# A vision-transformer block on one core: the order of the work in its first 45 microseconds is rearranged

## The chip, the cores and the metric

The kernel runs on one core of a Trainium2 chip. The core has a matrix engine (PE in the profile, with its weight loads as PEld), a vector engine (DVE, VectorE), a scalar engine (ACT, ScalarE), GpSimd (POOL) and a queue that only starts transfers (SP). The metric is the device time of one execution in microseconds; lower is better.

## The reference

The input is 16 images of 3 x 96 x 96. Each gives 36 patches of 768 values; with a class token an image has 37 rows of 256 values. Three steps follow. Only the first bears on this change.

```python
def tok(x, weight, class_token, pos_embedding):
    xn = patches * rsqrt(mean(patches * patches) + 1e-6)          # rms norm, per row
    scale = 127 / clip(max(abs(xn)), 1e-5)                        # per row
    xq = clip(round(xn * scale), -128, 127) / scale
    wscale = 1 / clip(mean(abs(weight)), 1e-5)                    # one number for all 256 x 768 weights
    wq = clip(round(weight * wscale), -1, 1) / wscale             # ternary weights
    return concat([class_token, xq @ wq.T]) + pos_embedding
h = tok(x)
h = h + attention(layernorm(h))        # 16 heads, rotary numerator, plain denominator, causal, + bout
h = h + mixture(layernorm(h))          # 8 heads of attention; one of 8 experts per row for values and outputs
```

## The kernel before

Every engine has its own program, written out by hand in order, and the engines meet in semaphores. The 592 rows (16 x 37) are worked in six groups of three images (111 rows; the last has one image). A group is one tile of `xp`, and group g is "g" everywhere below.

**The front (0 to 37 us).** SP starts all loads at once, in a fixed order: group 0, the identity (`ident`), group 1, the token weights `tw` (128 x 1536), groups 2 and 3, the other constants, the small vectors, groups 4 and 5, then the later weights. Per group:
- ScalarE squares and sums (`square`, L552), GpSimd makes the reciprocal root (`rrms`, a power, L451), VectorE takes the absolute maximum (`absmax`, L788), and from both VectorE makes the scales in three tiny steps (`quant_scales`, L801 to L805).
- ScalarE multiplies and rounds by adding a large number (`round_up`, L558). VectorE takes that number off again and clips into bf16 (`quantised`, L813). TensorE transposes the result (`turn_q`, L1153), ScalarE copies it out of PSUM (`quantised_T`, L567), TensorE multiplies with the ternary weights (`embed` on TensorE, L1164), and VectorE scales, adds the position row and takes the statistics of the layer norm (`embed` on VectorE, L836 to L819).
- GpSimd makes the reciprocal deviation (L471), VectorE normalises (`ln_apply`, L828), TensorE transposes (`turn_x`, L1173), ScalarE keeps a rounded copy (`x1_hi`, L572) and VectorE the remainder (`x1_lo`, L845).

The ternary weights need the sum of all absolute weights first: VectorE sums along each partition (L857), TensorE adds the 128 partitions (`total_job`, L1140), VectorE scales and clips `tw` in two passes (L862, L863), and ScalarE takes the rounding number off (L624, tile `tern`). No product of `embed` on TensorE starts before `tern`.

**After the front.** The first projection jobs (`proj_job`, L267 to L269) start between the last groups' `turn_x`, in the order of the list `START`. ScalarE copies their results out of PSUM (L597, L606), VectorE applies the rotary tables in four rounds (`rope`, L913 to L920), and from the second round on TensorE makes scores and the attention (L1249 to L1289). The mask of the numerator is added by a product: `keys_bf` (an identity placed twice, in bf16) times `ahead_bf` (L1249); VectorE makes both in `ahead`, ahead of the first `rope`. GpSimd adds the attention's output bias `bout` to `h` (L485), then makes the lower halves of the second stage's weights (`w2_lo`, L466), one after each round of `rope`; VectorE's `residual` (L966) waits for the bias to be in.

Of the kernel before, what the change touches and what calls it, by code (L numbers as in the profile page):

```python
# [9 lines left out]
ACT = mybir.ActivationFunctionType  # L10
AX = mybir.AxisListType.X
F32 = mybir.dt.float32
F32R = mybir.dt.float32r
BF16 = mybir.dt.bfloat16
# [99 lines left out]
def vit_block(nc, x, tokw, vecs, consts, wqkv, wout, w2, ve, oe, mask_rows, out):  # L114
    with ExitStack() as ctx:
# [9 lines left out]
        gate_sel = sbuf(ctx, "gate_sel", [NH2 * NE, NH2, DH2], F32R)  # L125
        ones = sbuf(ctx, "ones", [P, P])
        half_neg = sbuf(ctx, "half_neg", [P, GI])
        h = sbuf(ctx, "h", [R, G, D])
# [49 lines left out]
        ropex = sbuf(first, "ropex", [P, 2, QH])  # L178
        keys_bf = sbuf(first, "keys_bf", [P, 2, DH2], BF16)
        ahead_bf = sbuf(first, "ahead_bf", [P, 2 * KC * JS, S], BF16)  # L180
# [167 lines left out]
        def groups_of(t):  # L348

            return -(-min((t + 1) * P, T) // R)  # L350

        START = [("turn", 0), ("turn", 1), ("total", 0), ("bias", 0), ("turn", 2), ("embed", 0), ("turn", 3), ("embed", 1),
                 ("turn", 4), ("embed", 2), ("turn", 5), ("x", 0), ("embed", 3), ("x", 1), ("embed", 4), ("x", 2),
# [80 lines left out]
        def _(pool):  # L434
# [47 lines left out]

            pool.wait_ge(sm["x1lo_ready"], G)
            for g in range(G):
                pool.tensor_tensor(h[:, g], h[:, g], biasb[:, 1], ALU.add).then_inc(sm["h0b_ready"], 1)  # L485
            for n in range(4):
                pool.wait_ge(sm["rope_t"], RSTEPS * (n + 1))
                w2_lo(n)

            def ve_lo(e):  # L490
# [55 lines left out]
        def _(act):  # L546
# [70 lines left out]
            quantised_T(0)  # L617
            round_up(1)
            square(2)
            square(3)  # L620
# [3 lines left out]
            act.activation(tern[:], tw[:], ACT.Copy, bias=-ROUND).then_inc(sm["tern_ready"], 1)  # L624
            round_up(2)
            square(5)
            bias_rows()
            quantised_T(2)
            round_up(3)
            round_up(4)  # L630
            quantised_T(3)
            round_up(5)
# [144 lines left out]
        def _(dve):  # L777
# [53 lines left out]
            def embed(g):  # L831
                dve.wait_ge(sm["proj_ps"], g + 1)
                if g == 0:
                    dve.wait_ge(sm["bias_sb"], 1)
                    dve.wait_ge(sm["dqs_ready"], 1)
                step("h0_ready", dve.scalar_tensor_tensor(  # L836
                    out=h[:, g], in0=ps[0:R, 2 + g % 2, 0:D], scalar=dqs[:, g:g + 1], in1=biasb[:, 0],
                    op0=ALU.mult, op1=ALU.add))
                ln_stats(0, g)
# [7 lines left out]


            absmax(0)
            dve.wait_ge(ident_in, 16)  # L850
            dve.tensor_copy(ident_bf[:], cols("ident")).then_inc(sm["ident_ready"], 1)
            quant_scales([0])
            absmax(1)
            quantised(0)
            quant_scales([1])
            dve.wait_ge(tokw_in, 16)
            dve.tensor_reduce(small[:, 0:1], tw[:], AX, ALU.add, apply_absolute_value=True).then_inc(sm["wabs"], 1)  # L857
            quantised(1)
            dve.wait_ge(sm["tot_ps"], 1)
            step("wscale", dve.tensor_scalar(small[:, 1:2], ps[:, 6, 0:1], 1.0 / (D * DIN), Q_EPS, ALU.mult, ALU.max))  # L860
            step("wscale", dve.reciprocal(small[:, 2:3], small[:, 1:2]))
            step("clip_t", dve.tensor_scalar(tw[:], tw[:], small[:, 2:3], 1.0, ALU.mult, ALU.min))  # L862
            dve.tensor_scalar(tw[:], tw[:], -1.0, ROUND, ALU.max, ALU.add).then_inc(sm["tern_pre"], 1)  # L863
            absmax(2)
            quant_scales([2])
            absmax(3)
            quant_scales([3])
            quantised(2)
            step("wscale", dve.tensor_scalar(small[:, 3:4], small[:, 1:2], 1.0 / 127.0, None, ALU.mult))
            absmax(4)  # L870
            absmax(5)
            quant_scales([4, 5])
            dve.tensor_scalar(dqs[:], amc[:], small[0:R, 3:4], None, ALU.mult).then_inc(sm["dqs_ready"], 1)
            quantised(3)
            embed(0)
            quantised(4)
# [19 lines left out]
            def rope(r):  # L896
# [22 lines left out]
                for j in range(2):  # L919
                    many(dve.tensor_scalar(krot[:, c, im, DH2 * j:DH2 * j + S], tmp[:, 1], cols("par")[:, j:j + 1],  # L920
                                           None, ALU.mult))

            def ahead():

                dve.memset(keys_bf[:], 0.0).then_inc(sm["ahead_ready"], 1)
                dve.tensor_copy(ahead_bf[:], bcast(cols("ahead"), 1, 2 * KC * JS)).then_inc(sm["ahead_ready"], 1)
                dve.wait_ge(sm["ahead_ready"], 1)
                for r in range(RT):
                    rows = slice(r * P // RT, r * P // RT + S)
                    dve.tensor_copy(keys_bf[rows, :, 0:S],  # L930
                                    bcast(cols("ident")[rows, rows], 1, 2)).then_inc(sm["ahead_ready"], 1)

# [195 lines left out]
        def _(pe):  # L1128
# [55 lines left out]
            def proj_job(n):  # L1184
# [27 lines left out]
                ins.then_inc(sm["proj1_ps"], 1)  # L1212

            for what, n in START:
                if what == "turn":
                    turn_q(n)
                elif what == "total":
                    total_job()
                elif what == "bias":
                    bias_job()  # L1220
                elif what == "embed":
                    embed(n)
                elif what == "x":
                    turn_x(n)
                else:
                    proj_job(n)
# [371 lines left out]
```

## Time and profile before

| | us |
|---|---|
| median of three runs | 235.15 |
| the three runs | 233.58, 235.15, 235.27 |
| the profiled execution, its own time | 234.06 |
| its span, first to last instruction | 232.3 |
| PE busy in the span | 204.3 (88%) |
| DVE busy in the span | 175.1 (75%) |
| ACT busy, POOL busy | 93.4 (40%), 78.7 (34%) |

The profile is of one execution; the 1.76 us between its span and its own time lie around the instructions. Engine time counts as busy from an instruction's start to its end, so an engine that is busy 88% of the span is not at its peak. A row of the timeline gives start, duration, engine, line, operation and, in brackets, the idle time ahead of it and what ended that.

### The profile page before, as it was taken

The page shows a single profiled execution, that of the slowest core. Times are in us where ns is not written, and L with a number is a line of the kernel's source. Part 1 is how long each engine was busy: PE and PEld are TensorE (multiplying, and loading weights), DVE is VectorE, ACT ScalarE, POOL GpSimd, SP SyncE. Part 2 cuts the span into 40 slices and gives each one's busy share as a digit, 9 for nine tenths or more (in the row PEclk, how much of TensorE's full clock was granted, in tenths as well). Part 3 has the DMA queues.
Part 4 walks back from the last instruction along what each step waited for, and adds up shares of the span by engine and source line. Part 5 has one row for each costly group of instructions (what it writes and reads, how often), then busy time and mean ns, then how long its engine had stood idle before and what let it go on. Part 6 is the DMA issues. An engine that isn't in the chain of part 4 may idle for free.

```text
span 232.3 us, 5174 instructions
## 1 busy us (share of the span) xinstructions
PE 204.3 (88%) x2095; PEld 178.0 (77%) x2095; DVE 175.1 (75%) x320; ACT 93.4 (40%) x184; POOL 78.7 (34%) x82
## 2 busy tenths in 40 slices
PE   0153879979998999999999999999999999999994
PEld 0032759978785989977687787679989999899993
DVE  1679896998868669825466766676799979979972
ACT  3578837986643463453412606247003021110000
POOL 8552575422206124005065294767460000000000
PEclk9999988999999999999999999999999999999998
DMA  6999000000000200005320043094024425522003
GB/s 188 248 271 378 11 0 4 0 3 3 3 3 3 90 4 0 0 3 157 128 92 4 0 171 102 1 259 134 0 62 164 151 71 195 177 75 77 28 3 106
DMA packets 7183, 19.57 MB, mean 84 GB/s; under 512 B 1044, under 2 KB 1879, under 8 KB 7031
## 3 DMA queue, kind: packets, MB, share of 16 engines
q1 hardware_dynamic: 7158, 19.24, 26.3%
q8 instruction: 17, 0.28, 0.5%
q14 instruction: 8, 0.06, 0.1%
HBM read 18.55 MB, written 0.68 MB: 83 GB/s over the span
## 4 chain that ended last, share of the span: by engine, by line
PE 50%; DVE 29%; issue 8%; POOL 4%; ACT 4%; DMA 4%; SPq 1%; DVEq 0%; ACTq 0%; POOLq 0%
PE ps L267 12%; PE ps L268 11%; PE ps L269 11%; DVE gx L1117 8%; PE ps L1260 4%; DMA tw<-tok_weight 4%; PE ps L1473 2%; DVE oelo L1091 2%; DVE rden L947 2%; DVE amax L788 2%; PE ps L1443 1%; ACT ptb L734 1%; POOL velo L495 1%; PE ps L1276 1%; DVE stat L817 1%
## 5 line engine op out<-in xcount | busy, mean ns | idle before, releaser
L1117 DVE TENSOR_TENSOR gx<-maskb,oT 128x1184 fp32r<-128x1184 bf16 x31 | 42.3, 1410 | 0.6 <-PE ps L269 0.5
L1054 DVE COPY_PREDICATED v<-onehot,ps 128x512 f32<-128x512 uint8 (+3 forms) x40 | 25.7, 660 | 17.6 <-PE ps L269 17.3
L267 PE MATMUL ps<-gx,oelo 128*128 128x296 f32 x124 | 37.8, 305 | 0.6 <-DVE gx L1117 0.6
L269 PE MATMUL ps<-gx,oehi 128*128 128x296 f32 x124 | 37.2, 300 | 0.0
L268 PE MATMUL ps<-gx,oehi 128*128 128x296 f32 x124 | 36.9, 298 | 0.0
L267 PE MATMUL ps<-vehi,x2lo 128*128 128x512 f32 (+3 forms) x90 | 35.3, 392 | 0.0
L268 PE MATMUL ps<-velo,x2hi 128*128 128x512 f32 (+3 forms) x90 | 33.4, 371 | 0.0
L269 PE MATMUL ps<-vehi,x2hi 128*128 128x512 f32 (+3 forms) x90 | 33.2, 369 | 0.0
L495 POOL TENSOR_TENSOR velo<-veraw,vehi 128x1024 fp32r<-128x1024 f32 x8 | 19.1, 2390 | 20.4 <-ACT vehi L672 16.1
L267 PEld LDWEIGHTS ps<-gx,oelo 128*128 128x128 f32 x124 | 23.3, 188 | 1.8 <-issue 1.2
L268 PEld LDWEIGHTS ps<-gx,oehi 128*128 128x128 f32 x124 | 23.4, 189 | 0.0
L269 PEld LDWEIGHTS ps<-gx,oehi 128*128 128x128 f32 x124 | 23.3, 188 | 0.0
L267 PEld LDWEIGHTS ps<-vehi,x2lo 128*128 128x128 f32 (+1 forms) x90 | 16.2, 180 | 4.3 <-issue 0.7
L1153 PE MATMUL ps<-ident_bf,qb 111*128 111x111 bf16 x36 | 4.2, 282 | 17.2 <-DVE qb L813 17.2
L269 PEld LDWEIGHTS ps<-vehi,x2hi 128*128 128x128 f32 (+1 forms) x90 | 16.2, 180 | 3.7
L268 PEld LDWEIGHTS ps<-velo,x2hi 128*128 128x128 f32 (+1 forms) x90 | 16.2, 180 | 2.8
L1153 PEld LDWEIGHTS ps<-ident_bf,qb 111*128 111x128 bf16 x36 | 2.9, 131 | 18.9 <-DVE qb L813 18.8
L471 POOL TENSOR_TENSOR rstd<-lnv,half_neg 111x1 f32<-111x1 f32 x12 | 7.8, 649 | 24.7 <-DVE lnv L819 24.7
L742 ACT ACTIVATE oehi<-oeraw 128x1024 fp32r<-128x1024 f32 x8 | 8.5, 1064 | 18.9 <-DMA oeraw<-output_w 17.8
L721 ACT ACTIVATE pe<-sc 101x444 f32<-101x444 f32 (+1 forms) x6 | 3.2, 534 | 24.5 <-POOL sc L510 24.5
L267 PE MATMUL ps<-x2hi,w2lo 128*128 128x222 f32 (+1 forms) x32 | 10.4, 324 | 0.0
L947 DVE RECIPROCAL rden<-ps 128x296 f32<-128x296 f32 x4 | 8.0, 1991 | 3.1 <-PE ps L1289 3.1
(169 smaller groups left out, 471.5 us busy)
## 6 DMA issues: line engine op xcount, KB each, us to landing
maskb<-mask_rows SPq DMA_DIRECT2D x32, 148.0 KB, 3.5
veraw<-value_w SPq DMA_DIRECT2D x8, 512.0 KB, 3.6
oeraw<-output_w SPq DMA_DIRECT2D x8, 512.0 KB, 3.9
xp<-x_rows SPq DMA_DIRECT2D x6, 336.0 KB, 9.5
w2raw<-w_qkgate SPq DMA_DIRECT2D x1, 1088.0 KB, 14.8
tw<-tok_weight SPq DMA_DIRECT2D x1, 768.0 KB, 8.1
wqraw<-w_qkv SPq DMA_DIRECT2D x1, 768.0 KB, 12.7
out<-yo SPq DMA_DIRECT2D x4, 148.0 KB, 1.9
```

The lines of the kernel that those rows point to most:

```text
L267: pe.matmul(o, llo, rhi, start=start, stop=False)
L268: pe.matmul(o, lhi, rlo, start=False, stop=False)
L269: return pe.matmul(o, lhi, rhi, start=False, stop=stop)
L471: pool.tensor_tensor(rstd[:, which, g:g + 1], lnv[:, which, g:g + 1], half_neg[0:R, 0:1], ALU.pow).then_inc(sm["rstd_ready"], 1)
L495: pool.tensor_tensor(velo[:, e % NVR], veraw[:, e % NVR], vehi[:, e % NVR].bitcast(F32), ALU.subtract).then_inc(sm["velo_ready"], 1)
L742: act.activation(oehi[u % NOR][:], oeraw[RAW[u]][:], ACT.Copy).then_inc(sm["oehi_ready"], 1)
L788: dve.tensor_reduce(amax[:, g:g + 1], xp[0:R, g], AX, ALU.max, apply_absolute_value=True).then_inc(sm["amaxed"], 1)
L947: dve.reciprocal(rden[:], ps[:, DENB[b], 0:UN * S]).then_inc(sm["rden_ready"], 1)
L1054: dve.copy_predicated(v2[0:m, t, h0:h1], bcast(onehot[0:m, t, h0:h1, e], 2, DH2), ps[0:m, JBANK[n], 0:(h1 - h0) * DH2].rearrange("p (a b) ...
L1117: dve.tensor_tensor(gx[:, k % NGR].rearrange("p a b t -> p a (b t)"), bcast(maskb[:, w % NMR, k % MEU], 1, 2), oT[:, c % 2].bitcast(F32), ...
L1153: ins = pe.transpose(dst[:, c * (R + 1):c * (R + 1) + R], qb[:, g % NQB, c * P:(c + 1) * P], ident_bf[0:R, 0:R])
L1260: ins = pe.matmul(ps[0:QR, 2 * t + r, o:o + JS * S], key, qry, start=kind == 1, stop=kind == 1 or (ii, c) == (1, KC - 1))
```

## The change

- VectorE's sum of the absolute weights becomes a ScalarE pass (`Abs` with an accumulator) between `round_up(1)` and `square(2)`; its elementwise result goes into `tern`, which a later step overwrites.
- `absmax(2)` and `absmax(3)` move ahead of VectorE's wait for the total; the scales of groups 2 and 3 are made together; `quantised(3)` moves ahead of `embed(0)`, and `embed(0)` ahead of the scales of groups 4 and 5. `dqs` is made in two parts.
- On ScalarE `round_up(3)` moves to just behind `round_up(2)`, and `quantised_T(3)` to behind `quantised_T(2)`.
- `keys_bf` is made early, in a function of its own, `ahead_keys`, ahead of the scales of group 1.
- TensorE multiplies the identity by itself eight times behind the bias products, into a PSUM bank that nobody reads before it is written again; `embed(0)` comes ahead of `turn_q(2)`.
- GpSimd's six additions of `bout` move behind the four `w2_lo`, and no longer wait for `x1lo_ready`.

```diff
-        START = [("turn", 0), ("turn", 1), ("total", 0), ("bias", 0), ("turn", 2), ("embed", 0), ("turn", 3), ("embed", 1),
+        START = [("turn", 0), ("turn", 1), ("total", 0), ("bias", 0), ("warm", 8), ("embed", 0), ("turn", 2), ("turn", 3), ("embed", 1),
...
-            pool.wait_ge(sm["x1lo_ready"], G)
-            for g in range(G):
-                pool.tensor_tensor(h[:, g], h[:, g], biasb[:, 1], ALU.add).then_inc(sm["h0b_ready"], 1)
             for n in range(4):
                 pool.wait_ge(sm["rope_t"], RSTEPS * (n + 1))
                 w2_lo(n)
+            for g in range(G):
+                pool.tensor_tensor(h[:, g], h[:, g], biasb[:, 1], ALU.add).then_inc(sm["h0b_ready"], 1)
...
             round_up(1)
+            act.wait_ge(tokw_in, 16)
+            act.activation(tern[:], tw[:], ACT.Abs, accum_out=small[:, 0:1]).then_inc(sm["wabs"], 1)
             square(2)
...
             round_up(2)
+            round_up(3)
             square(5)
             bias_rows()
             quantised_T(2)
-            round_up(3)
+            quantised_T(3)
             round_up(4)
-            quantised_T(3)
             round_up(5)
...
+            def ahead_keys():
+                dve.memset(keys_bf[:], 0.0).then_inc(sm["ahead_ready"], 1)
+                dve.wait_ge(sm["ahead_ready"], 1)
+                for r in range(RT):
+                    rows = slice(r * P // RT, r * P // RT + S)
+                    dve.tensor_copy(keys_bf[rows, :, 0:S],
+                                    bcast(cols("ident")[rows, rows], 1, 2)).then_inc(sm["ahead_ready"], 1)
...
             quantised(0)
+            ahead_keys()
             quant_scales([1])
-            dve.wait_ge(tokw_in, 16)
-            dve.tensor_reduce(small[:, 0:1], tw[:], AX, ALU.add, apply_absolute_value=True).then_inc(sm["wabs"], 1)
             quantised(1)
+            absmax(2)
+            absmax(3)
             dve.wait_ge(sm["tot_ps"], 1)
...
             dve.tensor_scalar(tw[:], tw[:], -1.0, ROUND, ALU.max, ALU.add).then_inc(sm["tern_pre"], 1)
-            absmax(2)
-            quant_scales([2])
-            absmax(3)
-            quant_scales([3])
-            quantised(2)
+            quant_scales([2, 3])
             step("wscale", dve.tensor_scalar(small[:, 3:4], small[:, 1:2], 1.0 / 127.0, None, ALU.mult))
             absmax(4)
+            quantised(2)
+            dve.tensor_scalar(dqs[:, 0:4], amc[:, 0:4], small[0:R, 3:4], None, ALU.mult).then_inc(sm["dqs_ready"], 1)
+            quantised(3)
             absmax(5)
+            embed(0)
             quant_scales([4, 5])
-            dve.tensor_scalar(dqs[:], amc[:], small[0:R, 3:4], None, ALU.mult).then_inc(sm["dqs_ready"], 1)
-            quantised(3)
-            embed(0)
+            dve.tensor_scalar(dqs[:, 4:G], amc[:, 4:G], small[0:R, 3:4], None, ALU.mult).then_inc(sm["dqs_ready"], 1)
             quantised(4)
...
+            def keep_clock(n, bank):
+
+                for _ in range(n):
+                    pe.matmul(ps[:, bank, 0:P], cols("ident"), cols("ident"), start=True, stop=True)
```

`ahead()` keeps its place but makes only `ahead_bf`.

## Rows read from the trace of the kernel before

**Rows 1.** The chain of waits: start us, us, what
```profile
10.27 1.75 DVE small L857
...
19.79 1.82 DVE amax L788 x2
...
25.28 0.50 DVE h L836
...
41.22 1.31 DVE ropex L915
```

**Rows 2.** Timeline of ScalarE, front
```profile
10.01 0.94 ACT L558 ACTIVATE xp<-xp,qsc 111x768 f32<-111x768 f32 x1 [0.27 <-DVE qsc L805]
...
12.94 0.84 ACT L552 ACTIVATE sqjunk<-xp 111x768 f32<-111x768 f32 x1 [0.36 <-DMA xp<-x_rows]
...
15.68 0.84 ACT L552 ACTIVATE sqjunk<-xp 111x768 f32<-111x768 f32 x1 [1.19 <-DMA xp<-x_rows]
...
16.52 1.47 ACT L624 ACTIVATE tern<-tw 128x1536 bf16<-128x1536 f32 x1
17.90 0.92 ACT L558 ACTIVATE xp<-xp,qsc 111x768 f32<-111x768 f32 x1
```

**Rows 3.** Timeline of VectorE, front
```profile
9.37 0.21 DVE L801 TENSOR_SCALAR amc<-amax,rrms 111x1 f32<-111x1 f32 x1 [1.19 <-POOL rrms L451]
...
13.66 0.16 DVE L860 TENSOR_SCALAR small<-ps 128x1 f32<-128x1 f32 x1 [1.17 <-PE ps L1140]
...
15.11 0.96 DVE L863 TENSOR_SCALAR tw<-tw 128x1536 f32<-128x1536 f32 x1
...
21.71 0.34 DVE L801 TENSOR_SCALAR amc<-amax,rrms 111x1 f32<-111x1 f32 x2
...
22.61 0.55 DVE L813 TENSOR_SCALAR qb<-xp 111x768 bf16<-111x768 f32 x1
23.08 0.48 DVE L836 SCALAR_TENSOR_TENSOR h<-ps,dqs,biasb 111x256 f32<-111x256 f32 x1
...
24.35 0.56 DVE L813 TENSOR_SCALAR qb<-xp 111x768 bf16<-111x768 f32 x1
```

**Rows 4.** Timeline of GpSimd
```profile
14.24 1.86 POOL L451 TENSOR_TENSOR rrms<-msq,half_neg 111x1 f32<-111x1 f32 x1
...
37.66 4.22 POOL L485 TENSOR_TENSOR h<-h,biasb 111x256 f32<-111x256 f32 x6 [2.53 <-DVE x1lo L845]
...
58.40 1.34 POOL L466 TENSOR_TENSOR w2lo<-w2raw,w2hi 128x544 fp32r<-128x544 f32 x1 [3.78 <-DVE krot L920]
```

**Rows 5.** Timeline of TensorE
```profile
14.22 2.04 PE L1133 MATMUL ps<-vrow,cst 3*111 3x256 f32 x4 [0.60 <-DMA cst<-constants]
...
20.28 1.49 PE L1164 MATMUL ps<-tern,qT 128*111 128x256 bf16 x6
...
27.75 0.82 PE L1164 MATMUL ps<-tern,qT 128*111 128x256 bf16 x6
...
49.15 0.33 PE L1249 MATMUL ps<-ahead_bf,keys_bf 37*101 37x296 bf16 x2 [1.33 <-DVE krot L920]
```

**Rows 6.** Window: length; busy PE, PEld, DVE, ACT, POOL; granted clock; DMA share; GB/s
```profile
34.00:35.00 1.00, 1.00 (x6) 0.91 (x5) 0.95 (x4) 0.28 (x1) 0.54 (x1) 0.50 0.00 0
```

**Rows 7.** Timeline of VectorE from 35 us
```profile
35.17 0.41 DVE L828 TENSOR_SCALAR xhat<-h,mv,rstd 111x256 f32<-111x256 f32 x1
...
37.73 1.43 DVE L930 CAST keys_bf<-cst 37x74 bf16<-37x74 f32 x2
39.49 0.01 DVE L913 LOAD_MASK_SELECT partner<-ps  x1 [0.33 <-ACT kun L597]
```

**Rows 8.** Line L1173 of TensorE, timeline
```profile
36.68 0.36 PE L1173 MATMUL ps<-cst,xhat 111*128 111x111 f32 x2
```

**Rows 9.** VectorE's second rotary round and first residual, timeline
```profile
46.05 0.77 DVE L915 TENSOR_TENSOR ropex<-partner,cst 128x592 f32<-128x592 f32 x1
...
68.92 0.41 DVE L966 TENSOR_TENSOR h<-h,ps 111x256 f32<-111x256 f32 x1
```

More of the change, by code:

```diff
@@ L126, in vit_block @@
         ones = sbuf(ctx, "ones", [P, P])
+        keys_bf = sbuf(ctx, "keys_bf", [P, 2, DH2], BF16)
         half_neg = sbuf(ctx, "half_neg", [P, GI])
@@ L178, in vit_block @@
         ropex = sbuf(first, "ropex", [P, 2, QH])
-        keys_bf = sbuf(first, "keys_bf", [P, 2, DH2], BF16)
         ahead_bf = sbuf(first, "ahead_bf", [P, 2 * KC * JS, S], BF16)
@@ L835, in embed @@
                     dve.wait_ge(sm["dqs_ready"], 1)
+                elif g == 4:
+                    dve.wait_ge(sm["dqs_ready"], 2)
                 step("h0_ready", dve.scalar_tensor_tensor(
@@ L846, in x1_lo, with ahead @@
                                   hi.bitcast(F32), ALU.subtract).then_inc(sm["x1lo_ready"], 1)
+            def ahead():
+                dve.tensor_copy(ahead_bf[:], bcast(cols("ahead"), 1, 2 * KC * JS)).then_inc(sm["ahead_ready"], 1)
+            def ahead_keys():
[5 more added lines that the diff above has]
+                                    bcast(cols("ident")[rows, rows], 1, 2)).then_inc(sm["ahead_ready"], 1)
             absmax(0)
@@ L921, in rope @@
                                            None, ALU.mult))
[L923 to L931, printed above, removed]
             ahead()
@@ L1220, in _ @@
                     bias_job()
+                elif what == "warm":
+                    keep_clock(n, 4)
                 elif what == "embed":
```

## The prediction

> **What bounds the kernel now.** I read the chain of waits first, because this change shortens no large group of work: it reorders the front. The chain enters the front through VectorE's sum of the absolute weights at 10.27 us, stays on VectorE through the maxima of the groups and the additions of the embedding, and leaves through ScalarE's copies into VectorE's rotary rounds [rows 1]. Then I read the timelines of the engines next to each other, for what ends each pause. Two things decide the rest. ScalarE starts `tern` at 16.52, the moment its squares of group 4 are through, and those waited for group 4's transfer until 15.68 [rows 2]; VectorE had the clipped weights ready at 15.11 + 0.96 = 16.07 [rows 3]. So the weight path has 0.45 us of slack ahead of a transfer. And from 18 to 25 us ScalarE's rounding and VectorE's order hold each other up: the bf16 groups 3 and 4 come out at 22.61 and 24.35 only [rows 3], though ScalarE could round group 2 at 17.90 [rows 2].
>
> **The sum of the weights.** It leaves VectorE (1.75 us) [rows 1] for ScalarE. I price the pass by `tern`, which reads the same 128 x 1536 in 1.47 us [rows 2]. ScalarE is through with `round_up(1)` at 10.01 + 0.94 = 10.95, so the sum is there at about 12.45 (a little more for reading the accumulator), against 10.27 + 1.75 = 12.02 before. The total reached VectorE 1.64 us after the sum (13.66) [rows 3], with TensorE's transposes of group 1 in between; by that the new total arrives at the latest at 14.1. Now the two maxima ahead of that wait: group 3 landed at 12.94 [rows 2] and a maximum takes 1.82 / 2 = 0.91 [rows 1], so VectorE reaches the wait at 13.9. The clipping starts at 13.9 to 14.1 instead of 13.66 and ends 2.41 later, at 16.3 to 16.5. `tern` still starts at 16.52. Queued behind the pass on ScalarE are the squares of groups 2 and 3; they come 0.8 and 0.4 us later, and nothing needs them before 16.3. Gain of this part to here: nothing; group 4's transfer ends the wait in both orders.
>
> [...]
>
> **What follows from 16.5 us.** This is where the gain is. The joint scales of groups 2 and 3 take what those of 4 and 5 took together, 22.61 - 21.71 = 0.9 [rows 3], and need GpSimd's power for group 3. GpSimd's power beside the clipping took 1.86 us and ended with it at 16.10 [rows 4]; if it is held so again, until 16.5, the scales are there at 17.4, ahead of the end of `tern` (16.52 + 1.47 = 17.99). So ScalarE can run `round_up(2)` and `round_up(3)` back to back from 17.9, done at 18.8 and 19.75 at 0.92 each [rows 2]. VectorE: `quantised(2)`, then `quantised(3)` at 19.8 (before: 22.61), 0.55 to 20.35, `absmax(5)` to 21.25, `embed(0)` at 21.25 (before: 23.08) for 24.35 - 23.08 = 1.27, to 22.5 [rows 3]. But now the scales of groups 4 and 5 stand behind `embed(0)`: 22.5 + 0.9 = 23.4 at most, the part that ScalarE needs 0.1 earlier, so `round_up(4)` runs 23.3 to 24.2 and `quantised(4)` 24.2 to 24.75 (before: 24.35). `embed(1)` follows at 24.7; before it waited for TensorE until 25.28 [rows 1]. Of the 1.8 us at `embed(0)` 0.6 are left there; from there VectorE's loop of normalise, embed, statistics is the same as before. **Gain 0.6.**
>
> **The eight products.** They fill TensorE between the bias products' end, 14.22 + 2.04 = 16.26, and `embed(0)` [rows 5]. They are not in the trace. The nearest row is the bias, float32 as well: 512 columns in four records for 2.04. By columns the eight (1,024 columns) take 4.1 us, by records (16) 8.2, and at the doubled clock half of either: 2.0 to 8.2. I take 3 to 4, by columns with the clock risen on the way, for the rows are alike in that a column count sets them. They end at 19.3 to 20.3, `embed(0)` takes 0.82 at the high and 1.49 at the low clock [rows 5], and is done at 20.1 to 21.8; VectorE wants it at 21.25. Cost: nothing to 0.5; I take nothing, because `absmax(5)` covers it, and price the rest as a rival. `turn_q(2)` and `turn_q(3)`, now behind `embed(0)`, are needed by `embed(2)` after 25 us only.
>
> **The clock.** At 27.75 `embed` takes 0.82 and at 20.28 1.49, the ratio of 2.4 to 1.2 GHz [rows 5], though the clock column says full speed in both places; I go by the durations. In the window from 34 to 35 us the granted clock is 0.50, TensorE at 1.2 GHz under the first projection jobs [rows 6], after a stretch in which it only served `embed` group by group. Group 5 was normalised at 35.17 + 0.41 = 35.58 [rows 7], its transposes started at 36.68, behind those slow jobs [rows 8]: 1.1 us of the path. Forecast: the clock falls again, as TensorE's work from 25 to 32 us is unchanged, and this neither gains nor loses.
>
> **The mask's identity.** `keys_bf` (a memset and two casts, 1.43 together) leaves its place ahead of the rotary rounds. There it earns nothing by itself: VectorE waited another 0.33 for ScalarE's copy of the keys [rows 7]. In the new place it fills a pause of 1.19 [rows 3]; at 1.6 in all it would run 0.4 over, and the 0.4 goes into the weights' slack. The rotary rounds therefore follow ScalarE, which is 0.6 earlier.
>
> **The additions of `bout`.** Their six 0.7 us steps run from 37.66 to 41.88 [rows 4]. VectorE's L915, two operands from SBUF, starts at 41.22 and takes 1.31 on the chain [rows 1]; the same step of the next round, with GpSimd idle, takes 0.77 [rows 9]. The difference goes: **gain 0.5**, and TensorE, which paused 1.33 for VectorE at 49.15 [rows 5], can follow. In the new place the additions run behind the last `w2_lo` (58.40 + 1.34), to 64.0; `residual(0)` needs them at 68.92 [rows 4, 9], so 4.9 us of cover. VectorE reads PSUM beside them there. A second collision as large would cost 0.5; I take nought. `dqs` in two parts adds an instruction of some 0.2 in a pause: nought.
>
> **Sum.** 0.6 + 0.5 = 1.1 off the span: 232.3 to 231.2, and with the 1.76 around it 234.06 becomes 232.96. The median of the runs is 235.15, 1.1 above that execution, which would give 234.05. The two ends of the shown runs are as far apart as the gain, so I take the middle, 233.5.
>
> **Rivals**, each from the same middle of 234.6.
> - *The clock stays high into the projection jobs.* For it: eight products at the start of TensorE's work give it a rise earlier than 26 us; against it: the pauses from 25 to 32 remain. Up to 1.1 more, of which six products stand between the transposes anyway: 0.8. 232.7. The Trainium skill (TensorE: Matmul & The Clock Gate, "What's actually happening") says that the low clock is the default and activity releases it, which speaks for a rise at the eight products but not for its lasting.
> - *The eight products hold `embed(0)` up*, and the kernel is slower. Place: TensorE between 16.26 and `embed(0)`. At the middle of the two prices, 6.1 us, they end at 22.4, `embed(0)` near 23.5, and all that hangs on it is 2.2 later than in the forecast: 1.1 slower than before, 235.7. It decides from 21 us on: a later end than that takes the whole 1.1. Against it: TensorE is then busy from 14.2 without a pause, and under the projection jobs, just as dense, the clock rose again.
> - *Half of it does not arrive.* ScalarE's copies are only 0.6 earlier; if they and not VectorE set the first masked scores, the 0.5 is lost: 234.0. Against it: TensorE's 1.33 of waiting for VectorE.
>
> **How the numbers follow.** Forecast 0.56 (232.9 to 234.1), clock 0.18, half 0.16, slower 0.10. The range leaves out a tenth at each end: from 231.5, a little under the clock case counted from the profiled execution (234.06 - 1.1 - 1.1 = 231.9), to 235.8, which takes in the slow case's middle. A measurement here tells about 1% from no change; 1% below 235.15 is 232.8. Below it lies more than half of the clock case and a quarter of the forecast: 0.25. Above 237.5 lies only the end of the slow case: 0.06. Within: 0.69.
>
> **What would show it.** `tern` still at about 16.5; `quantised(3)` near 19.8; VectorE's first `embed` near 21.3 and the second near 24.7; L915 at 0.8 in both first rounds; `rope` starting 0.6 earlier, the first masked scores 1.1 earlier, and that distance kept to the end. I would be wrong if group 3 landed later than 13.2, for then the clipping waits for its maximum and `tern` moves one for one; if `Abs` brought a table load to ScalarE; or if the clock's rise and fall moved by more than the 1.1.

## The result, and the profile after

| us | before | changed |
|---|---|---|
| median (11 runs each) | 234.54 | 231.56 |
| lowest to highest | 232.92 to 237.74 | 230.99 to 234.74 |
| ratio of the two, 95% interval | | 0.9877 [0.9846, 0.9907] |

The kernel became 1.2% faster: 2.9 us, by the interval 2.2 to 3.6. The forecast was 1.1. Its direction was right and the time lies in its range, but the gain is more than twice the sum, and "faster by over 1%" had been given 0.25. Ratios, here and below, leave out executions that are more than 1.5% above the fastest of their kernel; medians and ranges take in all.

The profiled execution of the changed kernel is one of its longer ones (234.74 us, span 232.9), because TensorE ran at the low clock from 84 to 91 us, as shown below; up to 84 us its rows are held against those of before step by step.

The front first. ScalarE's timeline in the changed kernel answers to [rows 2]:

```profile
11.04 1.47 ACT L619 ACTIVATE tern<-tw 128x1536 bf16<-128x1536 f32 x1
12.41 0.19 ACT L619 ACTIVATION_READ_ACCUMULATOR tern<-tw 128x1 f32 x1
...
15.54 0.85 ACT L551 ACTIVATE sqjunk<-xp 111x768 f32<-111x768 f32 x1 [0.68 <-DMA xp<-x_rows]
16.41 1.48 ACT L625 ACTIVATE tern<-tw 128x1536 bf16<-128x1536 f32 x1
17.80 1.75 ACT L557 ACTIVATE xp<-xp,qsc 111x768 f32<-111x768 f32 x2
```

The new pass takes what `tern` takes. `tern` still starts when the squares of group 4 are through, and those still wait for a transfer: 16.41 against 16.52. Behind it the two roundings now stand together. VectorE's timeline, answering to [rows 3, 7] and to L915 on the chain of [rows 1]:

```profile
8.48 0.46 DVE L861 CAST keys_bf<-cst 37x74 bf16<-37x74 f32 x2
...
13.98 0.15 DVE L876 TENSOR_SCALAR small<-ps 128x1 f32<-128x1 f32 x1
15.42 0.96 DVE L879 TENSOR_SCALAR tw<-tw 128x1536 f32<-128x1536 f32 x1
19.58 0.56 DVE L814 TENSOR_SCALAR qb<-xp 111x768 bf16<-111x768 f32 x1
20.95 0.48 DVE L839 SCALAR_TENSOR_TENSOR h<-ps,dqs,biasb 111x256 f32<-111x256 f32 x1
24.50 0.48 DVE L839 SCALAR_TENSOR_TENSOR h<-ps,dqs,biasb 111x256 f32<-111x256 f32 x1
38.32 0.01 DVE L927 LOAD_MASK_SELECT partner<-ps  x1 [1.69 <-ACT kun L596]
39.85 0.78 DVE L929 TENSOR_TENSOR ropex<-partner,cst 128x592 f32<-128x592 f32 x1
```

`quantised(3)` comes at 19.58 (before 22.61), `embed(0)` at 20.95 (23.08), `embed(1)` at 24.50 (25.28): of 2.13 us, 0.78 are left at the second. The first rotary round, with GpSimd now idle beside it, takes 0.78 in the step that took 1.31 on the chain. TensorE's timeline:

```profile
16.02 3.51 PE L1221 MATMUL ps<-cst 128*128 128x128 f32 x16
19.37 0.82 PE L1168 MATMUL ps<-tern,qT 128*111 128x256 bf16 x6
35.51 0.35 PE L1177 MATMUL ps<-cst,xhat 111*128 111x111 f32 x2
55.73 1.04 PE L1287 MATMUL ps<-en,vblk 101*32 101x37 f32 x64
```

The eight products end at 19.53, and the first `embed` is over before VectorE wants it. The transposes of group 5 start at 35.51, not at 36.68 [rows 8], and the 64 attention products run in one piece. That last row has to be held against two of the kernel before, which the prediction had not read:

```profile
57.60 0.76 PE L1276 MATMUL ps<-en,vblk 101*32 101x37 f32 x63
58.87 0.19 PE L1276 MATMUL ps<-en,vblk 101*32 101x37 f32 x1 [0.50 <-issue]
```

There TensorE stood still for 0.50 us ahead of the last of the 64, and waited for nothing that the profile shows ("issue"). After it comes the second attention's denominator. VectorE's timeline, the first two denominators of the kernel before, then of the changed one:

```profile
58.40 1.95 DVE L947 RECIPROCAL rden<-ps 128x296 f32<-128x296 f32 x1
...
61.73 2.01 DVE L947 RECIPROCAL rden<-ps 128x296 f32<-128x296 f32 x1 [0.88 <-PE ps L1289]
```

```profile
56.53 1.95 DVE L951 RECIPROCAL rden<-ps 128x296 f32<-128x296 f32 x1
...
59.35 2.01 DVE L951 RECIPROCAL rden<-ps 128x296 f32<-128x296 f32 x1 [0.37 <-PE ps L1300]
```

They are 3.33 us apart before and 2.82 after.

Three windows of the changed kernel, answering to [rows 6]:

```profile
26.00:27.00 1.00, 0.61 (x7) 0.62 (x8) 1.00 (x3) 0.46 (x1) 1.00 (x2) 0.50 0.02 8
34.00:35.00 1.00, 0.63 (x5) 0.63 (x6) 0.86 (x3) 0.18 (x1) 0.67 (x1) 1.00 0.00 0
...
87.00:88.00 1.00, 1.00 (x5) 1.00 (x4) 0.97 (x2) 0.18 (x1) 0.20 (x1) 0.50 0.00 0
```

Full speed (2.4 GHz) is now granted under the first projection jobs, where it was 0.50 (1.2 GHz) before; but 0.50 came at 26 us, where TensorE serves `embed` group by group, and again at 84 to 91 us, under dense products that follow some pauses. Where the time went in this pair of profiles:

| step, start us | before | after | sum of gain |
|---|---|---|---|
| VectorE `embed(1)` | 25.28 | 24.50 | 0.78 |
| VectorE `embed(3)` | 29.24 | 28.83 | 0.41 |
| `x1_hi(5)` | 37.08 | 35.90 | 1.18 |
| `ropex` of the second round | 46.05 | 44.16 | 1.89 |
| first denominators | 58.40 | 56.53 | 1.87 |
| second denominators | 61.73 | 59.35 | 2.38 |
| first memset of `sc` | 87.30 | 84.89 | 2.41 |
| `gmT` of the first expert | 98.42 | 98.96 | -0.54 |

The order brings 0.78; the low clock under TensorE's `embed(3)` goes with a loss of 0.37; full clock under the projection jobs brings 0.77; the rotary round 0.5, and 0.2 more in the steps just ahead of it; the missing pause 0.5. Then the low clock at 84 us takes 2.95. Without that stretch this execution would have had some 234.06 - 2.41 = 231.65, close to the median of 231.56. So two things are to be settled: what the eight products do, and whether the clock is part of the change.

### The profile page after: what moved, and what is told of

It is laid out like the page before. It is cut to its first block, busy times and chain, and to the rows that moved or that the text cites. A ratio compares the mean times of both kernels' runs of the same rounds, so it can differ in the third digit from the quotient of the medians.

```text
span 232.9 us, 5208 instructions
## 1 busy us (share of the span) xinstructions
PE 208.2 (89%) x2111; PEld 182.3 (78%) x2111; DVE 171.9 (74%) x320; ACT 94.5 (41%) x186; POOL 78.5 (34%) x82
## 4 chain that ended last, share of the span: by engine, by line
PE 49%; DVE 25%; issue 8%; ACT 6%; DMA 4%; POOL 4%; SPq 2%; DVEq 0%; ACTq 0%; POOLq 0%
PE ps L267 12%; PE ps L268 11%; PE ps L269 11%; DVE gx L1121 8%; DMA xp<-x_rows 4%; PE ps L1271 4%; PE ps L1484 2%; DVE oelo L1095 2%; DVE rden L951 2%; PE ps L1454 1%; ACT ptb L735 1%; ACT xp L557 1%; DVE stat L818 1%; POOL velo L494 1%; PE ps L1287 1%
## 5 line engine op out<-in xcount | busy, mean ns | idle before, releaser
L1058 DVE COPY_PREDICATED v<-onehot,ps 128x512 f32<-128x512 uint8 (+3 forms) x40 | 25.7, 659 | 17.7 <-PE ps L269 17.4
L267 PEld LDWEIGHTS ps<-gx,oelo 128*128 128x128 f32 x124 | 23.3, 188 | 1.8 <-issue 1.3
L269 PEld LDWEIGHTS ps<-gx,oehi 128*128 128x128 f32 x124 | 23.3, 188 | 0.0
L1157 PE MATMUL ps<-ident_bf,qb 111*128 111x111 bf16 x36 | 3.4, 255 | 14.9 <-DVE qb L814 14.9
L466 POOL TENSOR_TENSOR w2lo<-w2raw,w2hi 128x544 fp32r<-128x544 f32 x4 | 5.4, 1352 | 17.7 <-DVE krot L934 17.7
L267 PE MATMUL ps<-x2hi,w2lo 128*128 128x222 f32 (+1 forms) x32 | 11.4, 355 | 0.0
```

What stands on the lines that cost most here:

```text
L267: pe.matmul(o, llo, rhi, start=start, stop=False)
L269: return pe.matmul(o, lhi, rhi, start=False, stop=stop)
L466: pool.tensor_tensor(w2lo[:, n // 2, part], w2raw[:, n // 2, part], w2hi[:, n // 2, part].bitcast(F32), ALU.subtract).then_inc(sm["w2lo_re ...
L1058: dve.copy_predicated(v2[0:m, t, h0:h1], bcast(onehot[0:m, t, h0:h1, e], 2, DH2), ps[0:m, JBANK[n], 0:(h1 - h0) * DH2].rearrange("p (a b) ...
L1157: ins = pe.transpose(dst[:, c * (R + 1):c * (R + 1) + R], qb[:, g % NQB, c * P:(c + 1) * P], ident_bf[0:R, 0:R])
```

## The experiments

Letters in the expectations: **theory A** says that the eight products earn by the clock under the projection jobs; **theory C** that they earn only because 32 more TensorE instructions (16 matmul records and their weight loads) move the pause. The rival to both is the prediction's sum, in which the products earn nothing. Each ratio is against the kernel before on the same chip. Since the low clock falls in different places from execution to execution, the place of each low stretch is told, and in places the lowest spans stand beside the medians. Diffs are against the changed kernel unless another is named; of a long list they show the part that changes, and `...` stands for lines left out.

**1. Without the eight products.**

```diff
-  ("total", 0), ("bias", 0), ("warm", 8), ("embed", 0), ("turn", 2),
+  ("total", 0), ("bias", 0), ("embed", 0), ("turn", 2),
```

> The changed kernel without the eight products. Theory A (the eight products decide where TensorE's clock is low later, and kept it high under the first projection jobs): the low stretch of some 3.4 us returns under the first two projection jobs, group 5's transposes come about 1 us later behind their normalised rows, and the time is 0.6 to 1.1 us above the changed kernel's, a ratio to the kernel before of 0.990 to 0.992. Theory B (the products only raise the clock for the first two embeddings, for which nothing waits; where the clock falls later is drawn anew in each execution): the time is within 0.3 us of the changed kernel's, a ratio of 0.987 to 0.989, and the low stretch is anywhere between 25 and 40 us.

Measured: 233.08 us, ratio 0.9888 [0.9856, 0.992], not told apart from the 0.9877 of the changed kernel. The clock was low at 25.1 to 28.5 us and full under the projection jobs, without the products. For the new order theory A falls by that. The pause in the attention products is back, and larger. TensorE's timeline of this kernel:

```profile
55.49 0.76 PE L1287 MATMUL ps<-en,vblk 101*32 101x37 f32 x63
57.05 0.19 PE L1287 MATMUL ps<-en,vblk 101*32 101x37 f32 x1 [0.80 <-issue]
```

From the first to the second denominators it takes 3.62 us; the changed kernel, 2.82. So the trace gives the products 0.80 here. Its shortest span is 229.6 and that of the changed kernel, on two chips, 229.1.

**2. The kernel before with the eight products alone** (diff against before):

```diff
-  ("bias", 0), ("turn", 2), ("embed", 0),
+  ("bias", 0), ("warm", 8), ("turn", 2), ("embed", 0),
...
```

> The kernel before, with nothing but the eight products added between the bias products and the transposes of group 2. Theory A: the clock is high under the first projection jobs, and the time falls by 0.6 to 1.1 us (ratio 0.995 to 0.997). Theory B: ratio 0.999 to 1.001, as the first embedding was not what VectorE waited for. In both, the products take about 3.5 us from 16.2 on and the first embedding then takes 0.82 instead of 1.49.

Measured: 234.14, ratio 0.9918 [0.9876, 0.9959], a larger gain than either theory had said, though the interval reaches theory A's. No pause; 2.80 us between the denominators, where the kernel before takes 3.33. The rotary step L915 still takes 1.27. The clock was low at 23.3 to 26.7 and 84.8 to 88.2, and full under the projection jobs. And VectorE's `embed(1)` comes at 24.52, which is not the pause's doing. Run 10 below is this kernel with products that do next to nothing, and its `tern` starts at the same time (15.77, here 15.74). TensorE's timeline here, then TensorE's and VectorE's of run 10:

```profile
22.86 0.47 PE L1153 MATMUL ps<-ident_bf,qb 111*128 111x111 bf16 x6 [2.11 <-DVE qb L813]
23.16 1.32 PE L1164 MATMUL ps<-tern,qT 128*111 128x256 bf16 x6
```

```profile
22.89 0.74 PE L1153 MATMUL ps<-ident_bf,qb 111*128 111x111 bf16 x6 [1.45 <-DVE qb L813]
23.42 1.49 PE L1164 MATMUL ps<-tern,qT 128*111 128x256 bf16 x6
...
24.95 0.48 DVE L836 SCALAR_TENSOR_TENSOR h<-ps,dqs,biasb 111x256 f32<-111x256 f32 x1 [0.37 <-PE ps L1164]
```

In the old order VectorE waits there for TensorE. The faster transposes and products save 0.43, the full clock under the projection jobs makes it 1.12 at `x1_hi(5)` (35.65 against 36.77), and 1.25 are left at the second denominators. In this pair, then, the products earn by the clock as well, as theory A says. In the new order TensorE is through with `embed(1)` at 21.43 in the changed kernel, three microseconds ahead of VectorE, and that wait is gone.

**3. The order alone**: no products, the additions of `bout` and `ahead_keys` in their old places.

```diff
-  ("bias", 0), ("warm", 8), ("embed", 0),
+  ("bias", 0), ("embed", 0),
...
+            pool.wait_ge(sm["x1lo_ready"], G)
+            for g in range(G):
+                pool.tensor_tensor(h[:, g], h[:, g], biasb[:, 1], ALU.add).then_inc(sm["h0b_ready"], 1)
             for n in range(4):
...
-            for g in range(G):
-                pool.tensor_tensor(h[:, g], h[:, g], biasb[:, 1], ALU.add).then_inc(sm["h0b_ready"], 1)
...
             quantised(0)
-            ahead_keys()
             quant_scales([1])
...
+            ahead_keys()
             ahead()
```

> The kernel before with only the order of the front changed: the sum of the weights on ScalarE, the maxima of groups 2 and 3, the joint scales and the orders of ScalarE, VectorE and the first embedding; no eight products, the mask's identity and the additions of bout in their old places. By my prediction's sum 0.6 to 0.8 us are gained at VectorE's second embedding (24.5 instead of 25.28) and nothing more: ratio 0.9965 to 0.9975, the step L915 of the first rotary round still at 1.3 us. Rival: the front's gain is given back by the first rotary round, which waits for ScalarE's copies: ratio 0.999 to 1.001.

Measured: 234.44, ratio 0.9938 [0.99, 0.9976]. `embed(1)` comes at 23.84, 1.44 before the kernel before; group 4 landed early here, and `tern` started at 15.62, 0.90 earlier. The rotary step takes 1.14, the pause 0.77; the clock was low at 85.3 to 88.7. The landing matters for the price of the order: with `tern` at 16.52 and 15.77 (run 10) the old order reaches `embed(1)` at 25.28 and 24.95 (0.33 for 0.75); the new one, with 16.41 and 15.63 (run 6), at 24.50 and 23.84 (0.66 for 0.78). So the new order is worth 0.7 to 0.8 where the group lands late, and 1.0 to 1.1 where it lands early.

**4. The additions of `bout` alone** (against before):

```diff
-            pool.wait_ge(sm["x1lo_ready"], G)
-            for g in range(G):
-                pool.tensor_tensor(h[:, g], h[:, g], biasb[:, 1], ALU.add).then_inc(sm["h0b_ready"], 1)
             for n in range(4):
                 pool.wait_ge(sm["rope_t"], RSTEPS * (n + 1))
                 w2_lo(n)
+            for g in range(G):
+                pool.tensor_tensor(h[:, g], h[:, g], biasb[:, 1], ALU.add).then_inc(sm["h0b_ready"], 1)
```

> The kernel before with only the additions of bout moved behind the four lower halves of the weights. By my prediction 0.5 us: the step with two SBUF operands in the first rotary round falls from 1.29 to 0.78, and the masked scores start 0.5 earlier: ratio 0.9975 to 0.9985. Rival (ScalarE's copies or TensorE's own jobs set the masked scores, so it does not arrive): ratio 1.000. A third possibility is a gain of 1.0 (ratio 0.9955 to 0.9965), if the pause of 0.50 that TensorE shows at 58.37 goes with it.

Measured: 234.32, ratio 0.9943 [0.9906, 0.9979]. VectorE's and TensorE's timelines of this kernel:

```profile
40.93 0.77 DVE L914 TENSOR_TENSOR ropex<-partner,cst 128x592 f32<-128x592 f32 x1
...
58.30 0.19 PE L1275 MATMUL ps<-en,vblk 101*32 101x37 f32 x1 [0.74 <-issue]
```

The step falls to 0.77. The second round is 0.80 earlier, of which 0.29 to 0.38 came from earlier transfers: 0.5 for the move, as forecast. But the pause is 0.74 here and takes 0.24 of it back. The clock was low at 33.0 to 36.4, as in the kernel before.

The ratios of runs 2, 3 and 4 make 0.8%, 0.6% and 0.6%, together more than the 1.2% of the whole change. On this chip single executions of the kernel before lay between 233.28 and 239.14. So the ratios are too coarse to price a part, and the prices here come from the traces.

**5. The changed kernel again**, as the control on the chip of the next three.

> The changed kernel as it is, on the chip of the three that follow, as their control: a ratio to the kernel before of 0.985 to 0.991, no pause of TensorE near 56 us, and the low stretches of the clock at other places than in the first profile.

Measured: 232.78, ratio 0.9904 [0.986, 0.9948]: by the ratio 2.2 us of gain (1.2 to 3.3), against 2.9 above. The clock was low at 25.7 to 29.1 and 83.7 to 90.5. No pause had been expected, and one of 0.31 is left. TensorE's timeline:

```profile
55.42 0.63 PE L1287 MATMUL ps<-en,vblk 101*32 101x37 f32 x47
56.37 0.34 PE L1287 MATMUL ps<-en,vblk 101*32 101x37 f32 x17 [0.31 <-issue]
```

It is 17 matmuls ahead of the end of the 64, where the kernel before had its own one matmul ahead of it: 16 matmuls and 16 weight loads earlier, which are the 32 instructions of the eight products. The denominators are 3.07 apart here.

**6. The products cut down to almost no work**: the same eight, each of 2 columns and 32 rows.

```diff
-                    pe.matmul(ps[:, bank, 0:P], cols("ident"), cols("ident"), start=True, stop=True)
+                    pe.matmul(ps[0:32, bank, 0:2], cols("ident")[:, 0:32], cols("ident")[:, 0:2], start=True, stop=True)
```

> The changed kernel with the eight products made tiny (32 rows by 2 columns instead of 128 by 128): as many instructions, hardly any work. Theory A (the products earn by the clock): it behaves like the kernel without products, the first embedding on TensorE takes about 1.49 instead of 0.82, and the pause of 0.5 to 0.8 us in the second round of attention products, which the profiles without products show just ahead of their last one, comes back. Theory C (they earn because 32 more instructions shift the place at which TensorE waits for nothing the profile shows): that pause stays away, though the first embedding runs at the low clock, and the time is that of the control within 0.3 us.

Measured: 231.58 (6 runs), ratio 0.9896 [0.9831, 0.9962]. TensorE's timeline of this kernel:

```profile
15.01 1.01 PE L1221 MATMUL ps<-cst 128*32 128x2 f32 x16
17.26 1.50 PE L1168 MATMUL ps<-tern,qT 128*111 128x256 bf16 x6 [1.23 <-ACT tern L625]
```

They take 1.01 instead of 3.51. `embed(0)` runs at the low clock, 1.50 against 0.82, and nothing later suffers: the following steps lie 0.2 to 0.5 ahead of the control's (`tern` started 0.46 earlier here), and the denominators stay 2.81 apart. In the new order what the eight products earn they earn by their number, as theory C says, and not by their work.

**7. The sum of the weights back on VectorE.**

```diff
             round_up(1)
-            act.wait_ge(tokw_in, 16)
-            act.activation(tern[:], tw[:], ACT.Abs, accum_out=small[:, 0:1]).then_inc(sm["wabs"], 1)
...
             quant_scales([1])
+            dve.wait_ge(tokw_in, 16)
+            dve.tensor_reduce(small[:, 0:1], tw[:], AX, ALU.add, apply_absolute_value=True).then_inc(sm["wabs"], 1)
             quantised(1)
```

> The changed kernel with the sum of the absolute weights back on VectorE, ahead of the bf16 rows of group 1. By my prediction the pass costs VectorE 1.75 us ahead of two maxima that now stand in front of the total, so the clipping ends at about 16.9 instead of 16.4 and the ternary weights come 0.4 to 0.8 later (more where group 4 lands early); all that follows is later by that: 0.4 to 0.8 us above the control. Rival: ScalarE's freed 1.6 us bring the squares earlier and make up for it: within 0.2 us of the control.

Measured: 231.98, ratio 0.9903 [0.9867, 0.994]; by the medians not told apart from the control. In the trace `tern` starts at 16.78, against 16.09 in the control, and the 0.69 is kept to the first denominators; 0.47 is left after them. VectorE's timeline, and one row of ScalarE's:

```profile
10.44 1.75 DVE L871 TENSOR_REDUCE small<-tw 128x1 f32<-128x1536 f32 x1 [0.47 <-DMA tw<-tok_weight]
...
15.79 0.96 DVE L879 TENSOR_SCALAR tw<-tw 128x1536 f32<-128x1536 f32 x1
```

```profile
15.72 0.85 ACT L551 ACTIVATE sqjunk<-xp 111x768 f32<-111x768 f32 x1 [0.71 <-DMA xp<-x_rows]
```

With the two maxima ahead of the clipping as well, it ends at 15.79 + 0.96 = 16.75, 0.69 later than in the control, and `tern` waits for it. But group 4 also landed later in this execution: its squares start at 15.72 (15.16 in the control), and since `tern` came 0.84 behind them in the kernel before [rows 2], it could not have started before about 16.56 here. So 0.2 of the 0.69 is the sum on VectorE, and 0.5 the landing. The ScalarE pass keeps the clipping out of the way of `tern`; what that is worth hangs on the landing.

**8. `keys_bf` back in its old place.**

```diff
             quantised(0)
-            ahead_keys()
             quant_scales([1])
...
+            ahead_keys()
             ahead()
```

> The changed kernel with the mask's identity made again just ahead of the rotary rounds. By my prediction it earns nothing by its place: VectorE waits 1.7 us there for ScalarE's copy of the keys, and the three instructions take 0.6 to 1.5: time within 0.2 us of the control, first rotary round at the same distance behind ScalarE's copy. Rival: the casts run over the wait, 0.3 to 0.6 us above the control.

Measured: 232.22, ratio 0.992 [0.9875, 0.9966], within 0.3 us of the control in the trace. VectorE's timeline:

```profile
36.01 0.42 DVE L861 CAST keys_bf<-cst 37x74 bf16<-37x74 f32 x2
37.81 0.01 DVE L926 LOAD_MASK_SELECT partner<-ps  x1 [1.03 <-ACT kun L596]
```

The casts stand in a wait for ScalarE's copy, and 1.03 of that is left behind them. The move earns nothing, as forecast. With GpSimd idle they take 0.42, not the 1.43 of [rows 7].

**9. The small products of 6, and six fillers** (128 x 128) in the stretch ahead of 84 us, where TensorE has pauses. If the low clock at 84 us goes with them, it should be gone.

```diff
-  ("qk", 7), ("gate", 0), ("turn", 4), ("gate", 1), ("turn", 5),
+  ("qk", 7), ("fill", 3), ("gate", 0), ("fill", 2), ("turn", 4), ("gate", 1), ("fill", 1), ("turn", 5),
...
+  elif kind == "fill":
+      for _ in range(n):
+          pe.matmul(ps[:, 5, 0:P], cols("ident"), cols("ident"), start=True, stop=True)
```

> The changed kernel with two further edits: its eight products tiny, as in the earlier run, and six float32 products of the identity by itself (three ahead of the first gate job, two ahead of the transposes of group 4, one ahead of group 5's), in pauses of TensorE between 79 and 83 us, into a bank that holds nothing there. The tiny products should cost nothing against the changed kernel. If TensorE's thin work there is what lets the clock fall at 84 us (worth some 3 us where it happens, as in three of four profiles on the last chip), the low stretch at 84 to 91 us is seen more rarely and the median falls by 0.5 to 1.5 us below the control's; the fillers may hold the transposes up by 0.1 to 0.4. Rival: the fall comes as before and the time is 0.2 to 0.4 above the control's.

Measured: 231.9 (6 runs, 231.62 to 232.84), ratio 0.9869 [0.9828, 0.9909]. The profile has no low stretch behind the front. One window of this kernel, then the same of the control:

```profile
84.00:85.00 1.00, 1.00 (x9) 0.99 (x9) 0.69 (x2) 0.55 (x3) 0.36 (x1) 1.00 0.00 0
```

```profile
84.00:85.00 1.00, 1.00 (x6) 1.00 (x7) 0.56 (x2) 0.49 (x3) 0.23 (x1) 0.50 0.00 0
```

The fillers cost 0.5 (third denominators 0.19 ahead of those of run 6, `sc` memset 0.35 behind). The best run is 0.7 above the control's best, which ran on another chip. None of the six runs is above 232.84, while four of the control's twelve are above 234.3; with six runs, one profile and two chips this is a hint and no proof. At the medians this version is not told apart from the changed kernel.

**10. The kernel before with the small products alone** (the edit of 2, with the products of 6).

> The kernel before with nothing but the eight tiny products added. Theory C (the place of TensorE's pause in the second round of attention products hangs on the count of its instructions): the pause of 0.50 goes, the second reciprocal of the denominators starts 0.5 earlier against the first, and the time falls by 0.5 us, ratio 0.997 to 0.999. Theory A: nothing moves, the pause stays at 0.5 and the ratio is 1.000.

Measured: 233.5, ratio 0.9946 [0.9907, 0.9986]. TensorE's timeline and one window:

```profile
57.32 1.11 PE L1283 MATMUL ps<-en,vblk 101*32 101x37 f32 x64
```

```profile
34.00:35.00 1.00, 1.00 (x6) 0.89 (x6) 0.86 (x4) 0.00 (x0) 0.67 (x1) 0.50 0.00 0
```

The 64 are in one piece, the denominators 2.89 apart (3.33), while the clock under the projection jobs is as low as in the kernel before. So eight products that do next to nothing move the pause in the old kernel too. The trace gives them 0.44; the ratio says 1.3 (0.3 to 2.2), more than the 0.5 expected, but with 0.44 in its interval.

**11. Twenty-four products** instead of eight, for the rival that had them hold `embed(0)` up.

```diff
-  ("warm", 8)
+  ("warm", 24)
```

> The changed kernel with 24 products of the same size in place of eight. My prediction's slow rival, made real: the products end at about 23 instead of 19.4 us, VectorE's first embedding starts at 23.8 instead of 20.9, the second 2.6 later, and the time is 2.2 to 2.7 us above the changed kernel's, as late as the kernel before or later. Rival: the group loop behind them catches up, under 1 us above the changed kernel's.

Measured: 235.12, ratio 1.0012 [0.9982, 1.0043]. TensorE's and VectorE's timelines:

```profile
16.66 8.51 PE L1221 MATMUL ps<-cst 128*128 128x128 f32 x48
...
25.87 0.48 DVE L839 SCALAR_TENSOR_TENSOR h<-ps,dqs,biasb 111x256 f32<-111x256 f32 x1 [4.28 <-PE ps L1168]
```

`embed(0)` comes 4.9 us later than with eight, `embed(1)` at 29.41, and 2.25 us of it arrive at the `sc` memset, compared with the kernel before. The rival's mechanism is real, and the count decides: eight lie under the wait for `tern`, twenty-four do not. Here the products ran mostly at the low clock, which made the delay larger than expected.

**12. The kernel before, unchanged**, for where its clock falls.

> The kernel before, as it is, for its profile: ratio 0.997 to 1.003. The pause of TensorE near 58 us is there again, as it goes with the instructions; whether the low stretch of the clock lies under the first projection jobs again is open: if it does, the order of the front decides it, if not, it is drawn.

Measured: 235.87, ratio 1.0035 [0.9994, 1.0075]. The pause is at the same instruction, 0.47. The windows of this execution:

```profile
34.00:35.00 1.00, 0.54 (x5) 0.41 (x4) 0.82 (x5) 0.04 (x1) 0.67 (x1) 1.00 0.00 0
...
49.00:50.00 1.00, 1.00 (x15) 1.00 (x15) 0.97 (x2) 0.03 (x1) 0.38 (x1) 0.50 0.08 16
```

Full clock under the projection jobs, in the kernel before, and low from 48.3 to 55.1 and 89.3 to 92.7 instead. Where the low stretch falls varies between executions of one and the same kernel. But it is not without a pattern: of the four profiles with the old order and no products of full size, three are low from 33 us (before, runs 4 and 10), and of the other ten none. Of the nine with the new order five are low from about 84 us on, and of those four none. So the change may well move the low stretch, gaining under the projection jobs and losing at 84 us; fourteen profiles don't settle it.

## Why the prediction was right in direction and too small

The time lies 0.06 above the lower end of the range, and that end had been set by the rival in which the products keep the clock high. So that the range held is luck; the account goes by the terms.

- **The front up to `tern`: right.** The pass took 1.47 and 0.19 for its accumulator, the total arrived at 13.98 (13.9 to 14.1 said), the clipping ended at 16.38 (16.3 to 16.5), `tern` started at 16.41. Run 7 shows what the pass is for, and that it was worth 0.2 there.
- **The order: mechanism right, size 0.1 to 0.5 low.** `quantised(3)` 19.58 (19.8 said), `embed(0)` 20.95 (21.3), `embed(1)` 24.50 (24.7). The term of 0.6 was worked out for the one landing of group 4 in the profile; it measures 0.7 to 0.8 there and 1.0 to 1.1 at an early one.
- **The additions of `bout`: right.** 0.5 in run 4 and in the changed kernel. They ran from 57.83 to 62.00 in the new place. The Trainium skill (GPSIMD Engine Reference, "8. Key points") says that GpSimd shares its SBUF interfaces with VectorE, and that there is contention with VectorE instructions that have two SBUF inputs or run in a two-port mode. The trace agrees: the rotary step, with two SBUF inputs, went from 1.31 [rows 1] to 0.78. The casts of `keys_bf` went from 1.43 to 0.46; they have one input, and no row shows their mode.
- **The eight products: the step that failed.** "Cost: nothing to 0.5; I take nothing" looked only at what they hold up at the front. Their 3.51 us were as priced and cost nothing, though the clock did not rise on the way but at their end: most of the sixteen records follow each other at 213 ns, the last at 110. What was left out is that 32 more instructions in TensorE's stream change where it pauses 40 us later. By the distance of the denominators that earned 0.3 to 0.5 against the kernel before (2.80 to 3.07 in the kernels with eight products, 3.33 before), and 0.5 to 0.8 against the changed kernel without them (3.62; runs 1, 2, 5, 6, 10). The pause stood in the trace of before as a row of its own, and the prediction did not read it.
- **The clock: "falls again" was right, "neither gains nor loses" is not shown.** In this pair of profiles it gave 0.77 at the projection jobs, took 0.37 at `embed` and 2.95 at 84 us. As a mean, on the chip of runs 5 to 8, the granted clock was 0.986 over twelve executions of the changed kernel and 0.994 over 29 of the kernel before: there it took rather than gave. In the rival the products keep the clock high under the projection jobs. In the new order they are not needed for that (runs 1, 6 and 9 have it without them), and the kernel before can have it too (run 12). In the old order one pair of profiles speaks for the rival (run 2 against run 10).
- **"Half of it does not arrive": refuted.** The first masked scores are 1.88 earlier, the second rotary round 1.89.

**The sum as it should have been:** 0.7 to 1.1 for the order, 0.5 for the rotary round, 0.3 to 0.5 for the pause: 1.5 to 2.1; with the 0.2 ahead of the rotary round that no run singled out, 1.7 to 2.3, and the clock left out. The shortest spans differ by 2.0 to 2.3 (229.1 against 231.1 to 231.4 on three chips; 2.3 on the one where both were run), and the two ratios give 2.9 [2.2, 3.6] and 2.2 [1.2, 3.3]. What the first has beyond 2.3 is within its interval.

**What the pause is.** It hangs on the number of instructions ahead of it: that is shown. Counted in the traces, eleven of the fourteen have a gap among these 64 products, and each time TensorE goes on with its 962nd recorded instruction, whichever the kernel. The Trainium skill (Runtime: NRT & Kernel Launch, "Instruction fetch mechanics") says that instructions come in blocks of 256 and that crossing into the next is mostly hidden. Here the traces bear out the fetch, and at this crossing it is not hidden. They hold DMA packets of 16 KB for instructions, about one for every 256 that TensorE records. Their line on the page of the kernel before, then the window in which one of them starts:

```profile
q8 instruction: 17, 0.28, 0.5%
```

```profile
56.00:57.00 1.00, 1.00 (x32) 0.98 (x23) 0.96 (x2) 0.10 (x1) 0.00 (x0) 1.00 0.07 16
```

This packet starts at 56.30 and has landed at 57.47; TensorE goes on at 58.87, 1.40 later. In all eleven traces it goes on 1.25 to 1.50 after such a landing, and in the three without a gap the packet was there in time (1.34, 1.47 and 2.72 ahead). The size follows from when the packet starts: 0.7 to 1.3 us ahead of the 64 products without the eight, 1.4 to 2.0 with eight, 3.5 with twenty-four. No run moved the packet by itself, so this is a reading of the traces.

**What stays open.** The runs do not show what sets the start of that packet, where the changed kernel's clock falls as a rule, and what decides in which execution it falls at 84 us.

## What to carry to other kernels

Read every "issue" pause on the chain of the kernel before: instructions added upstream move it (0.3 to 0.8 us here), so an edit "off the path" can earn or cost half a microsecond far behind its place, and a few tiny instructions test that cheaply. Work out a gain of reordering for more than one landing of the transfer that it hangs on. When single executions differ by more than the change, compare step by step up to the first stretch of different clock, and the shortest spans beside the medians.

## What the runs showed of the hardware

- A pause of TensorE at one number in its instruction stream, the 962nd recorded: 0.50 and 0.47 us in two executions of the kernel before, 0.74, 0.77 and 0.80 in three kernels without the products (runs 4, 3, 1). With eight products it stands 16 matmuls earlier in the work: 0.31 and 0.27 in runs 5 and 8, and too short for a row of its own in the others. It ends 1.25 to 1.50 us after a 16 KB instruction packet has landed.
- The granted clock can fall to 0.50 under dense products: in the changed kernel TensorE was busy for 0.75 and 0.81 of the windows at 80 and 81 us and for 0.99 and more of the next two, then the clock was low from 84 to 91 us, which cost 2.95 us. With six products in the pauses ahead of it, it was absent from the one profile taken.
- Two casts of 37 x 74 took 1.43 us beside GpSimd's additions and 0.42 to 0.46 without.
- The clock column can't be trusted at the start: `embed(0)` of run 6 took 1.50, 1.8 times the 0.82 of the changed kernel, while the column reads full speed.
